# Where a phase's extremes are multiplied and reduced in a chain of selective scans

## The chip, the cores and the metric

The kernel runs on one core of a Trainium2 chip. The time is the device time of one execution in microseconds, and the median of several executions is what counts. All data are 32-bit floats.

## What is computed

The reference takes `x` (32 sequences of 750 steps with 64 channels) through three state-space layers, then an attention block and a mixture of 16 experts. Only the layers matter here. Cut down:

```python
def _ssm_layer(x, A_log, Dp, W_dbc, W_dt, b_dt):
    A = -jnp.exp(A_log)
    dbc = jnp.einsum('ble,ce->blc', x, W_dbc)
    delta, Bm, Cm = jnp.split(dbc, [DT_RANK, DT_RANK + N_STATE], axis=-1)
    delta = jax.nn.softplus(jnp.einsum('blr,er->ble', delta, W_dt) + b_dt)
    dA = jnp.exp(delta[..., None] * A)
    dBx = (delta * x)[..., None] * Bm[:, :, None, :]
    ...
    y = jnp.einsum('blen,bln->ble', hs, Cm)
    return y + Dp * x
```

`hs` is the scan `h = dA * h + dBx` along the sequence, for 64 states per channel; behind each of the first two layers pairs of neighbouring steps are averaged.

## The kernel before, in words

Two sequences at a time lie on the 128 partitions (64 channels each). A **unit** is 750 columns of such a pair (748 in layer 2). There are 28 units, grouped into 8 **phases** of four units (two in the last two phases): phases 0 to 3 are layer 0, 4 and 5 layer 1, 6 and 7 layer 2.

States whose decay is so strong that `exp` gives zero need no scan: their sum is one quadratic form of the input. For each phase the kernel finds out which states those are. It needs the smallest delta of the phase, and so the **extremes** of the first projection (row 0 of `W_dbc`): TensorE multiplies half units (375 columns) by `w0pm`, whose columns hold the projection and its negative (`extreme_rows`, matmul at L515), VectorE reduces to a maximum per partition (`extremes`, L1320), TensorE transposes that column into one row (`extremes_row`, L573), VectorE reduces it (`extremes_of_row`, L1325 and L1326), TensorE spreads it (`extremes_spread`, L577), and `lowest`, ScalarE's `bounds`, `classes` and `picks` follow. The slow states that are left, up to two, are scanned; a loop for more (`more_slots`) is skipped at run time when there are none.

The work on a unit n, by engine:

- TensorE: `mixed` (the quadratic form's product, L493 and L494 with `quad`), `summed` (a sum over channels of `PT`, L493 and L494 with `work,packed`), `weighted_b` (the mixed input B x for scan j into `pairs[1 + j]`, L493 and L494 with `big,work`), `rows` (the rows of C for unit n+1 and of delta for unit n+3 into `bank[0]`, L530 and L536), `sums` (the pooled sum of both scans, L566).
- VectorE: `load` (L1379, mixed input by `u`), `product` (L1358), `by_delta` (L1364), the scan `recur` (L1386), `output` (L1371), `read` (L1398, state by the row of C), each for 750 columns; `load`, `recur` and `read` twice a unit.
- ScalarE: softplus in parts (L965 to L979), `decay` (L990, one for each scan), `rows_out` (L1034, the rows from `bank[0]` to SBUF), `sums_out` (L1041).
- GpSimd: the rest of delta, `u`, and the pooled sums.
- SyncE: for each unit it writes the rows to DRAM (L399) and reads them back, spread over 64 partitions: `z_row` (L408) for delta, `c_rows` (L415) for C.

Each engine works its own list in the order in which `period(n)` writes it, once for n = -2 to 27; semaphores tie the lists together, and a waiting instruction holds everything behind it on its engine. PSUM is four pairs of two banks: `bank[0]` and `bank[1]` are pair 0 (`bank[0]` serves the rows and all small products of the phase chain), `pairs[1]` and `pairs[2]` hold the two scans, `pairs[3]` the quadratic form. Before, `extreme_rows` wrote into `pairs[1]`, which scan 0 of the next unit needs too.

`chain(n)` gives for a unit n the phase p that comes next and the place q of n in its own phase. With q = 0 (units 0, 4, 8, 12, 16, 20) the extremes of the next phase are made in that period; q = 1 and q = 2 carry the rest of the chain. `new` says that n is the first unit of a phase other than the first. In a new period TensorE's list opened with

```python
                if new:
                    pe.wait_ge(more_v, MV[last_of(n - 1) + 1])
                    summed(n + 1)
```

and in a period with q = 0 it went on, behind the rows, with

```python
                if q == 0:
                    pe.wait_ge(hc_v, STATIC * n + 1)
                    extreme_rows(p, pairs[1]).then_inc(dec_p, 1)
                    pe.wait_ge(rw_a, EVENT_AT[n + 1])
                ...
                if q == 0:
                    extremes_row(p)
                    weighted_b(n + 1, 0)
```

`extremes_row` waits for VectorE's reduction, so `weighted_b(n + 1, 0)`, and `mixed(n + 2)` behind it, did too.

Of the kernel before, what the change touches and what calls it, by code (L numbers as in the profile page):

```python
# [81 lines left out]
def program(nc, a, out):  # L82
    SCALE = float(D) ** 0.25
    with ExitStack() as ctx:
# [33 lines left out]
        w0pm = sb("w0pm", [128, LAYERS, 32])  # L118
# [370 lines left out]
        def _(pe):  # L489
# [19 lines left out]
            def extreme_rows(p, dst):  # L509
# [4 lines left out]
                for i in range(2 * U):  # L514
                    mm = pe.matmul(dst[32 * (i % 4):32 * (i % 4) + 32, 512 * (i // 4):512 * (i // 4) + w],  # L515
                                   w0pm[:, l, :], xcols(l, c + i * w, w), start=True, stop=True)
                return mm

            def rows(k):
# [3 lines left out]
                if c_of is not None and c_of >= Z_OF:  # L523
                    extreme_rows(NP - 1, bank[0]).then_inc(rw_p, 1)
                    return
# [6 lines left out]
                if s_of is not None:  # L532
                    _, l, w, x = unit(s_of)
                    x_ready(s_of)
                    for c in range(2):
                        mm = pe.matmul(bank[0][64 + 32 * c:96 + 32 * c, 0:w // 2], w0pm[:, l, :],  # L536
# [87 lines left out]
            def period(n):  # L624
# [7 lines left out]
                if new:  # L632
                    pe.wait_ge(more_v, MV[last_of(n - 1) + 1])
                    summed(n + 1)
# [16 lines left out]
                if nxt and not new:  # L651
                    summed(n + 1)
                if old is not None:
                    sums(old, 0)
                if q == 0:
                    pe.wait_ge(hc_v, STATIC * n + 1)
                    extreme_rows(p, pairs[1]).then_inc(dec_p, 1)
                    pe.wait_ge(rw_a, EVENT_AT[n + 1])
                elif q == 1:
# [5 lines left out]
                if s is not None:  # L665
                    pe.wait_ge(rw_a, EVENT_AT[n + 1])
                    extreme_rows(s, pairs[1]).then_inc(dec_p, 1)
# [15 lines left out]
                if nxt and q != 0:  # L683
# [11 lines left out]
                if q == 0:  # L695
                    extremes_row(p)
                    weighted_b(n + 1, 0)
# [568 lines left out]
        def _(v):  # L1266
            v.sem_inc(more_v, 1)

            def setup():
# [6 lines left out]
                for k in range(2):  # L1276
                    blk = slice(64 * k, 64 * k + 64)
                    v.tensor_copy(w0pm[blk, :, k], w0[blk, :])
                    v.tensor_scalar(w0pm[blk, :, 2 + k], w0[blk, :], -1.0, None, ALU.mult)
# [31 lines left out]
            def extremes(p):  # L1311
                l, _, U = PHASES[p]
                w = WIDTH[l] // 2
                if p == NP - 1:
                    v.wait_ge(rw_a, EVENT_AT[LAST - 1])
                    src = bank[0][:, 0:w]
                else:
                    v.wait_ge(dec_p, DP[p] + 1)
                    src = pairs[1][:, :].rearrange("p (b t) -> p b t", b=2)[:, 0:U // 2, 0:w]
                v.tensor_reduce(smx[:, :], src, AXX if p == NP - 1 else AXXY, ALU.max).then_inc(dec_v, 1)  # L1320

            def extremes_of_row(p):
                v.wait_ge(dec_p, DP[p] + 2)
                row = bank[0][0:1, 0:128].rearrange("p (g c) -> p g c", c=32)
                v.tensor_reduce(sext[:, 0:1], row[:, :, 0:2], AXXY, ALU.max, negate=True)  # L1325
                v.tensor_reduce(sext[:, 1:2], row[:, :, 2:4], AXXY, ALU.max).then_inc(dec_v, 1)  # L1326
# [105 lines left out]
            def period(n):  # L1432
# [35 lines left out]
                elif nxt:  # L1468
                    by_delta(n + 1)
                if here:  # L1470
                    recur(n, 1)
                if q == 0:
# [464 lines left out]
```

## Time and profile before

| | us |
|---|---|
| median of 3 executions | 789.09 (788.72 to 789.63) |
| the profiled execution, its own time | 790.49 |
| its span, first to last instruction | 788.7 |
| TensorE busy in the span | 713.2 (90%) |
| VectorE busy in the span | 545.3 (69%) |
| ScalarE busy in the span | 425.2 (54%) |
| GpSimd busy in the span | 439.4 (56%) |
| mean granted TensorE clock | 0.968 of full |

Busy shares are means over the whole span: the scans take the first 330 us or so, the attention and the experts the rest. Lines in the profile are lines of the kernel before. Of a 32-bit product the trace holds two passes, so a matmul of the program stands there as two (x2). Starts of instructions in the timeline overlap the ends of the ones ahead on the same engine by some tenths of a microsecond, so the distance from start to start is what a step takes.

### The profile page before, as it was taken

The page shows a single profiled execution, that of the slowest core. Times are in us where ns is not written, and L with a number is a line of the kernel's source. Part 1 is how long each engine was busy: PE and PEld are TensorE (multiplying, and loading weights), DVE is VectorE, ACT ScalarE, POOL GpSimd, SP SyncE. Part 2 cuts the span into 40 slices and gives each one's busy share as a digit, 9 for nine tenths or more (in the row PEclk, how much of TensorE's full clock was granted, in tenths as well). Part 3 has the DMA queues.
Part 4 walks back from the last instruction along what each step waited for, and adds up shares of the span by engine and source line. Part 5 has one row for each costly group of instructions (what it writes and reads, how often), then busy time and mean ns, then how long its engine had stood idle before and what let it go on. Part 6 is the DMA issues. An engine that isn't in the chain of part 4 may idle for free.

```text
span 788.7 us, 11097 instructions
## 1 busy us (share of the span) xinstructions
PE 713.2 (90%) x3474; PEld 355.5 (45%) x3474; DVE 545.3 (69%) x859; ACT 425.2 (54%) x763; POOL 439.4 (56%) x402
## 2 busy tenths in 40 slices
PE   5689998989989895848999999889999999999997
PEld 2335444544545452326777777623333333333332
DVE  3389899999999898585588888485444444454543
ACT  1678777878687874543545554443434334343332
POOL 1368777877877765735666666233444344443440
PEclk9699999999999998688999999989999999999999
DMA  4346554434545553124000000552954334443400
GB/s 130 126 122 155 152 147 124 131 83 121 129 121 123 125 134 81 39 62 86 1 2 4 3 4 4 109 107 55 209 108 99 82 83 105 106 92 79 97 1 20
DMA packets 30098, 70.20 MB, mean 89 GB/s; under 512 B 4483, under 2 KB 20175, under 8 KB 29647
## 3 DMA queue, kind: packets, MB, share of 16 engines
q1 hardware_dynamic: 29727, 68.77, 36.7%
q8 instruction: 31, 0.51, 0.3%
q10 hardware_dynamic: 304, 0.63, 0.2%
q14 instruction: 36, 0.29, 0.1%
HBM read 66.96 MB, written 2.43 MB: 88 GB/s over the span
## 4 chain that ended last, share of the span: by engine, by line
PE 46%; DVE 8%; issue 1%; ACT 1%; DVEq 0%; ACTq 0%
PE pair L834 22%; PE pair L915 11%; PE pair L775 4%; PE pair L758 3%; PE pair L811 2%; PE pair L798 1%; DVE big L1526 1%; PE pair L820 1%; PE pair L826 1%; DVE big L1530 1%; DVE big L1592 0%; DVE big L1591 0%; DVE big L1538 0%; DVE big L1531 0%; DVE big L1846 0%
## 5 line engine op out<-in xcount | busy, mean ns | idle before, releaser
L1689 DVE TENSOR_TENSOR hidden<-pair,tmp 128x502 f32<-128x502 f32 (+1 forms) x192 | 121.6, 675 | 130.1 <-PE pair L834 105.2
L1820 POOL TENSOR_TENSOR hidden<-xs,big 128x502 f32<-128x502 f32 (+1 forms) x96 | 111.8, 1166 | 166.0 <-PE pair L834 145.7
L1242 ACT ACTIVATE tmp<-pair 128x502 f32<-128x502 f32 (+1 forms) x192 | 102.4, 586 | 157.0 <-PE pair L834 157.0
L1846 POOL TENSOR_TENSOR big<-big 94x512 f32<-94x512 f32 (+3 forms) x120 | 89.2, 777 | 56.5 <-DVE big L1591 56.5
L834 PE MATMUL pair<-xs,w 64*128 64x502 f32 (+1 forms) x384 | 107.1, 634 | 0.0
L834 PE MATMUL pair<-hidden,w 64*128 64x502 f32 (+1 forms) x384 | 98.7, 590 | 4.0 <-DVE hidden L1689 3.1
L1386 DVE TENSOR_TENSOR_SCAN pair<-tmp,pair 128x750 f32<-128x750 f32 (+1 forms) x56 | 95.9, 1712 | 0.4
L1711 POOL TENSOR_TENSOR big<-big,work 128x750 f32<-128x750 f32 (+1 forms) x28 | 45.7, 1632 | 88.7 <-ACT big L973 88.7
L915 PE MATMUL pair<-hidden,w 128*64 128x502 f32 (+1 forms) x384 | 92.3, 603 | 0.0
L493 PE MATMUL pair<-big,work 128*128 128x512 f32 x112 | 61.3, 629 | 2.8 <-DVE work L1398 2.8
L834 PEld LDWEIGHTS pair<-hidden,w 64*128 64x128 f32 x384 | 36.8, 188 | 51.1 <-issue 46.5
L834 PEld LDWEIGHTS pair<-xs,w 64*128 64x128 f32 x384 | 29.2, 185 | 66.1 <-issue 36.6
L1379 DVE TENSOR_TENSOR pair<-pair,big 128x750 f32<-128x750 f32 (+1 forms) x56 | 52.1, 930 | 1.4 <-PE pair L494 0.5
L915 PEld LDWEIGHTS pair<-hidden,w 128*64 128x64 f32 x384 | 23.7, 138 | 63.3 <-DVE hidden L1689 34.6
L990 ACT ACTIVATE tmp<-big,picked 128x749 f32<-128x749 f32 (+2 forms) x56 | 49.6, 909 | 2.5 <-issue 2.4
L1714 POOL TENSOR_TENSOR work<-work 128x750 f32<-128x750 f32 (+1 forms) x28 | 46.2, 1649 | 3.0 <-ACT work L979 3.0
L1721 POOL TENSOR_TENSOR big<-big 128x750 f32<-128x750 f32 (+1 forms) x28 | 46.7, 1667 | 1.7 <-issue 0.9
L1716 POOL TENSOR_TENSOR big<-big,work 128x750 f32<-128x750 f32 (+1 forms) x28 | 46.1, 1646 | 2.2
L775 PEld LDWEIGHTS pair<-big 93*120 93x120 f32 (+1 forms) x384 | 42.2, 184 | 2.9 <-issue 1.2
L775 PE MATMUL pair<-big 93*120 93x65 f32 (+1 forms) x384 | 42.6, 268 | 0.0
L811 PE MATMUL pair<-big 120*64 120x188 f32 x384 | 34.1, 326 | 6.7 <-issue 3.8
L493 PE MATMUL pair<-big,quad 128*128 128x512 f32 x56 | 32.6, 666 | 6.4 <-DVE work L1371 5.4
(189 smaller groups left out, 1241.3 us busy)
## 6 DMA issues: line engine op xcount, KB each, us to landing
big<-dispatched SPq DMA_DIRECT2D x40, 502.0 KB, 6.6
spread<-rowsd SPq DMA_DIRECT2D x48, 375.0 KB, 5.7
spread<-rowsd SPq DMA_DIRECT2D x48, 187.5 KB, 3.4
big<-in_x SPq DMA_DIRECT2D x12, 375.0 KB, 6.3
big<-dispatched SPq DMA_DIRECT2D x8, 498.0 KB, 5.8
spread<-rowsd SPq DMA_DIRECT2D x8, 374.0 KB, 4.9
w<-in_w SPq DMA_DIRECT2D x5, 512.0 KB, 7.0
big<-in_x SPq DMA_DIRECT2D x1, 1500.0 KB, 7.2
```

Of the source, the lines that this page charges most:

```text
L493: pe.matmul(dst[:, 0:512], lhsT, rhs[:, 0:512], start=True, stop=True)
L775: mm = pe.matmul(bank[4 + n % 2][0:FT, at:at + 65], kF[r % 2][0:rows, unit, FT * f:FT * f + FT], qkv[r % 2][0:rows, unit, 143:208], start= ...
L811: mm = pe.matmul(dst[64 * b:64 * b + 64, TOK * k:TOK * k + TOK], kvm[n % 2][:, k, FTN * b + f, :], qT[n % 2][:, f, TOK * b:TOK * b + TOK], ...
L834: pe.matmul(dst[:, 0:hi - lo], weights[blk, HID * e:HID * e + HID], x[blk, :], start=True, stop=True)\
L915: mm = pe.matmul(bank[4][64 * b:64 * b + 64, 0:hi - lo], w3[:, e, :], hidT[(2 * expert + b) % 8][:, 0:hi - lo], start=(e == 0), stop=(e == ...
L990: act.activation(seqs(dA[j], l)[:, :, 1:], seqs(of(delta, n), l)[:, :, 1:], ACT.Exp, scale=picked[p % 2][:, j:j + 1]).then_inc(dk_a, 1)
L1242: act.activation(sT[i % 4][:, 0:w], bank[BANK1[i]][:, 0:w], ACT.Silu).then_inc(silu_a, 1)
L1379: v.tensor_tensor(bu, bu, of(u, n), ALU.mult).then_inc(bu_v, 1)
L1386: v.tensor_tensor_scan(h, dA[j][:, 0:w], h, 0.0, ALU.mult, ALU.add).then_inc(sc_v, 1)
L1689: v.tensor_tensor(hidT[i % 8][:, 0:hi - lo], bank[BANK2[i]][:, 0:hi - lo], sT[i % 4][:, 0:hi - lo], ALU.mult)\
L1820: pool.tensor_tensor(xw[e % 4][:, 0:hi - lo], xs[:, lo:hi], wx[:, e, 0:hi - lo], ALU.mult)\
L1846: ins = eng.tensor_tensor(dst[:, :, at:at + H * m].rearrange("p u (h d) -> p u h d", d=m), t[:, :, :, 0:m], t[:, :, :, k:D], ALU.mult)
```

## The change

The table `w0pm` grows from 32 to 34 columns a layer. The projection now stands in columns 2 and 3, its negative in 6 and 7. Read from column 2 on, a product gives rows 0, 1 (projection) and 4, 5 (negative); read from column 0 on, rows 2, 3 and 6, 7. `extreme_rows` uses that: the first four half units of a phase go to the four quarters of 32 partitions of `bank[0]` with the first form, the other four are added into the same quarters with the second. All eight half units then lie in one bank of 375 columns, eight rows a quarter, where before they lay in two banks, 750 columns, four rows a quarter. The reduction and the one behind it read accordingly.

TensorE's list: `extreme_rows` in a period with q = 0 now waits until ScalarE has copied the rows out of `bank[0]`; `weighted_b(n + 1, 0)` goes ahead of `extremes_row`; in a new period with q = 0 `rows` goes ahead of `summed(n + 1)`. VectorE's list: with q = 0 `by_delta(n + 1)` moves behind the second scan.

```diff
-        w0pm = sb("w0pm", [128, LAYERS, 32])
+
+        w0pm = sb("w0pm", [128, LAYERS, 34])
...
-            def extreme_rows(p, dst):
+            def extreme_rows(p):
+
                 l, c, U = PHASES[p]
                 w = WIDTH[l] // 2
                 for n in range(UB[p], UB[p + 1]):
                     x_ready(n)
                 for i in range(2 * U):
-                    mm = pe.matmul(dst[32 * (i % 4):32 * (i % 4) + 32, 512 * (i // 4):512 * (i // 4) + w],
-                                   w0pm[:, l, :], xcols(l, c + i * w, w), start=True, stop=True)
+                    at = 2 - 2 * (i // 4)
+                    mm = pe.matmul(bank[0][32 * (i % 4):32 * (i % 4) + 32, 0:w], w0pm[:, l, at:at + 32],
+                                   xcols(l, c + i * w, w), start=(i < 4), stop=(i >= 2 * U - 4))
                 return mm
...
                 if new:
                     pe.wait_ge(more_v, MV[last_of(n - 1) + 1])
-                    summed(n + 1)
+                    if q != 0:
+                        summed(n + 1)
...
-                if nxt and not new:
+                if nxt and (not new or q == 0):
                     summed(n + 1)
                 if old is not None:
                     sums(old, 0)
                 if q == 0:
-                    pe.wait_ge(hc_v, STATIC * n + 1)
-                    extreme_rows(p, pairs[1]).then_inc(dec_p, 1)
                     pe.wait_ge(rw_a, EVENT_AT[n + 1])
+                    extreme_rows(p).then_inc(dec_p, 1)
...
-                if nxt and q != 0:
+                if nxt:
                     weighted_b(n + 1, 0)
...
                 if q == 0:
                     extremes_row(p)
-                    weighted_b(n + 1, 0)
...
-                    v.tensor_copy(w0pm[blk, :, k], w0[blk, :])
-                    v.tensor_scalar(w0pm[blk, :, 2 + k], w0[blk, :], -1.0, None, ALU.mult)
+                    v.tensor_copy(w0pm[blk, :, 2 + k], w0[blk, :])
+                    v.tensor_scalar(w0pm[blk, :, 6 + k], w0[blk, :], -1.0, None, ALU.mult)
...
-                    src = bank[0][:, 0:w]
                 else:
                     v.wait_ge(dec_p, DP[p] + 1)
-                    src = pairs[1][:, :].rearrange("p (b t) -> p b t", b=2)[:, 0:U // 2, 0:w]
-                v.tensor_reduce(smx[:, :], src, AXX if p == NP - 1 else AXXY, ALU.max).then_inc(dec_v, 1)
+                v.tensor_reduce(smx[:, :], bank[0][:, 0:w], AXX, ALU.max).then_inc(dec_v, 1)
...
                 if k == 1:
                     classes(NP - 1)
-                elif nxt:
+                elif nxt and q != 0:
                     by_delta(n + 1)
                 if here:
                     recur(n, 1)
+                if q == 0:
+                    by_delta(n + 1)
                 if q == 0:
                     extremes(p)
```

TensorE's list at the first period of phase 1 (unit 4). `work,packed` is `summed`, `rowsel` and `w0pm ... x2` the rows, `w0pm ... x8` the extremes, `big,work` the mixed input, `packed,smx` is `extremes_row`, `big,quad` is `mixed`. Before:

```order
L493 MATMUL pair<-work,packed 128x512
L494 MATMUL pair<-work,packed 128x238
L530 MATMUL pair<-big,rowsel 32x375 x2
L536 MATMUL pair<-big,w0pm 32x375 x2
L515 MATMUL pair<-big,w0pm 32x375 x8
L573 MATMUL pair<-packed,smx 1x128
L493 MATMUL pair<-big,work 128x512
L494 MATMUL pair<-big,work 128x238
L493 MATMUL pair<-big,quad 128x512
L494 MATMUL pair<-big,quad 128x238
```

The same place now, where the lines of the kernel have moved by one to three:

```order
L533 MATMUL pair<-big,rowsel 32x375 x2
L539 MATMUL pair<-big,w0pm 32x375 x2
L494 MATMUL pair<-work,packed 128x512
L495 MATMUL pair<-work,packed 128x238
L518 MATMUL pair<-big,w0pm 32x375 x8
L494 MATMUL pair<-big,work 128x512
L495 MATMUL pair<-big,work 128x238
L576 MATMUL pair<-packed,smx 1x128
L494 MATMUL pair<-big,quad 128x512
L495 MATMUL pair<-big,quad 128x238
```

Two things moved: the rows are ahead of `summed`, and the mixed input is ahead of `extremes_row`. At unit 0 only the second did.

VectorE's list at the same period, from the first `read` (`tmp<-pair,spread`) to the output (`work<-pair,packed,big`); L1386 is the scan. Before:

```order
L1398 TENSOR_TENSOR tmp<-pair,spread 128x750
L1364 TENSOR_TENSOR pair<-pair,big 128x750
L1386 SCALAR_TENSOR_TENSOR pair<-tmp,pair 128x750
L1320 TENSOR_REDUCE smx<-pair 128x1
L1371 SCALAR_TENSOR_TENSOR work<-pair,packed,big 128x750
```

The same place now:

```order
L1398 TENSOR_TENSOR tmp<-pair,spread 128x750
L1386 SCALAR_TENSOR_TENSOR pair<-tmp,pair 128x750
L1364 TENSOR_TENSOR pair<-pair,big 128x750
L1320 TENSOR_REDUCE smx<-pair 128x1
L1371 SCALAR_TENSOR_TENSOR work<-pair,packed,big 128x750
```

`by_delta` has gone behind the scan.

## Rows read from the trace of the kernel before

**Rows 1.** The page, busy tenths of the span in 40 slices.
```profile
DVE  3389899999999898585588888485444444454543
...
PEclk9699999999999998688999999989999999999999
```

**Rows 2.** Table by stretch: length, busy us (instructions) by engine, clock, DMA.
```profile
107.00:310.00 203.00, 186.79 (x740) 95.58 (x739) 189.59 (x225) 152.00 (x243) 153.49 (x113) 1.00 0.48 120
```

**Rows 3.** Waits of VectorE by cause: us in total, times, longest us.
```profile
DVE work L1398 <- DMA spread<-rowsd: 6.9, 6, 2.0
```

**Rows 4.** The tile `smx`: durations in ns (min/median/max), and who waited for L1320.
```profile
L1320 DVE TENSOR_REDUCE smx<-pair x8: 520/911/937, 18.4 to 303.9; 128x1 f32<-128x750 f32 x6, 128x1 f32<-128x374 f32 x2
...
  PE pair L573: 11.9, 7
```

**Rows 5.** Timeline at unit 0: start us, us, engine, line [idle before, releaser].
```profile
41.86 0.93 DVE L1398 TENSOR_TENSOR tmp<-pair,spread 128x750 f32<-128x750 f32 x1
...
42.84 1.47 PE L515 MATMUL pair<-big,w0pm 128*32 128x375 f32 x16
...
43.63 0.95 DVE L1364 TENSOR_TENSOR pair<-pair,big 128x750 f32<-128x750 f32 x1 [0.84 <-POOL big L1716]
...
47.17 0.38 PE L573 MATMUL pair<-packed,smx 128*1 128x128 f32 x2 [2.86 <-DVE smx L1320]
...
49.19 1.91 PE L493 MATMUL pair<-big,quad 128*128 128x512 f32 x2
...
51.93 0.94 DVE L1358 TENSOR_TENSOR work<-pair,big 128x750 f32<-128x750 f32 x1 [1.55 <-PE pair L494]
...
55.49 0.93 DVE L1398 TENSOR_TENSOR work<-pair,spread 128x750 f32<-128x750 f32 x1
```

**Rows 6.** The tile `spread`, C rows of unit 1, then unit 5's.
```profile
L415 SPq DMA_DIRECT2D spread<-rowsd x2: 597/597/597, 45.1 to 45.7; - x2
...
DMA to landing us min/median/max: 4.8/5.3/5.8
...
DMA to landing us min/median/max: 5.3/6.2/7.2
```

**Rows 7.** Timeline at unit 4 and the start of unit 5.
```profile
85.32 1.02 PE L493 MATMUL pair<-work,packed 128*128 128x512 f32 x2
...
86.67 0.51 PE L530 MATMUL pair<-big,rowsel 128*32 128x375 f32 x2
...
86.69 0.92 ACT L990 ACTIVATE tmp<-big,picked 128x749 f32<-128x749 f32 x1 [0.70 <-issue]
...
86.78 0.95 DVE L1364 TENSOR_TENSOR pair<-pair,big 128x750 f32<-128x750 f32 x1 [0.80 <-PE pair L494]
...
87.57 0.48 ACT L1034 ACTIVATE rows<-pair 128x375 f32<-128x375 f32 x1
...
87.65 1.72 DVE L1386 TENSOR_TENSOR_SCAN pair<-tmp,pair 128x750 f32<-128x750 f32 x1
...
90.34 0.38 PE L573 MATMUL pair<-packed,smx 128*1 128x128 f32 x2 [1.57 <-DVE smx L1320]
...
92.02 1.02 PE L493 MATMUL pair<-big,quad 128*128 128x512 f32 x2
...
92.22 0.95 DVE L1379 TENSOR_TENSOR pair<-pair,big 128x750 f32<-128x750 f32 x1
...
93.47 0.94 DVE L1358 TENSOR_TENSOR work<-pair,big 128x750 f32<-128x750 f32 x1 [0.31 <-PE pair L494]
...
99.15 0.94 DVE L1398 TENSOR_TENSOR work<-pair,spread 128x750 f32<-128x750 f32 x1 [2.03 <-DMA spread<-rowsd]
```

**Rows 8.** Timeline, ScalarE's row copies at units 8 and 20.
```profile
131.41 0.48 ACT L1034 ACTIVATE rows<-pair 128x375 f32<-128x375 f32 x1 [0.18 <-PE pair L536]
...
258.96 0.48 ACT L1034 ACTIVATE rows<-pair 128x375 f32<-128x375 f32 x1 [0.20 <-PE pair L536]
```

**Rows 9.** Timeline, ScalarE before the first unit.
```profile
20.39 1.00 ACT L967 ACTIVATE work<-spread,packed,wdtc 128x750 f32<-128x750 f32 x1
```

More of the change, by code:

```diff
@@ L523, in rows @@
                 if c_of is not None and c_of >= Z_OF:
-                    extreme_rows(NP - 1, bank[0]).then_inc(rw_p, 1)
+                    extreme_rows(NP - 1).then_inc(rw_p, 1)
                     return
@@ L535, in rows @@
                     for c in range(2):
-                        mm = pe.matmul(bank[0][64 + 32 * c:96 + 32 * c, 0:w // 2], w0pm[:, l, :],
+                        mm = pe.matmul(bank[0][64 + 32 * c:96 + 32 * c, 0:w // 2], w0pm[:, l, 2:34],
                                        x[:, w // 2 * c:w // 2 * c + w // 2], start=True, stop=True)
@@ L666, in period @@
                     pe.wait_ge(rw_a, EVENT_AT[n + 1])
-                    extreme_rows(s, pairs[1]).then_inc(dec_p, 1)
+                    extreme_rows(s).then_inc(dec_p, 1)
                     extremes_row(s)
@@ L1315, in extremes @@
                     v.wait_ge(rw_a, EVENT_AT[LAST - 1])
-                    src = bank[0][:, 0:w]
                 else:
                     v.wait_ge(dec_p, DP[p] + 1)
-                    src = pairs[1][:, :].rearrange("p (b t) -> p b t", b=2)[:, 0:U // 2, 0:w]
-                v.tensor_reduce(smx[:, :], src, AXX if p == NP - 1 else AXXY, ALU.max).then_inc(dec_v, 1)
+                v.tensor_reduce(smx[:, :], bank[0][:, 0:w], AXX, ALU.max).then_inc(dec_v, 1)
             def extremes_of_row(p):
                 v.wait_ge(dec_p, DP[p] + 2)
-                row = bank[0][0:1, 0:128].rearrange("p (g c) -> p g c", c=32)
-                v.tensor_reduce(sext[:, 0:1], row[:, :, 0:2], AXXY, ALU.max, negate=True)
-                v.tensor_reduce(sext[:, 1:2], row[:, :, 2:4], AXXY, ALU.max).then_inc(dec_v, 1)
+                row, U = bank[0][0:1, 0:128].rearrange("p (g c) -> p g c", c=32), PHASES[p][2]
+                v.tensor_reduce(sext[:, 0:1], row[:, :, 0:U], AXXY, ALU.max, negate=True)
+                v.tensor_reduce(sext[:, 1:2], row[:, :, 4:4 + U], AXXY, ALU.max).then_inc(dec_v, 1)
             def lowest(p):
```

## The prediction

> **What bounds the kernel now.** The page comes first. In the 40 slices VectorE stands at 8 or 9 tenths from the third slice up to about 310 us, which is the stretch of the scans; behind that it falls to half, and nothing of the change lies there [rows 1]. The table by stretch says it with numbers: from 107 to 310 us VectorE is busy 189.59 of 203 us, TensorE 186.79, at a granted clock of 1.00 [rows 2]. So in the scans VectorE's own list of work sets the pace, and what can be won is (a) work taken off VectorE and (b) the few stretches in which it stands. Among its waits by cause stands one on the DMA that spreads the C rows, before `read`: 6.9 us in 6 times, the longest 2.0 us [rows 3]. A few large waits make up such a sum, so I looked for each of them in the timeline.
>
> The instruction that the change is about is the reduction of a phase's extremes, L1320: 8 times, 911 ns in the middle and 520 ns at its shortest; TensorE waited for it 11.9 us in 7 times [rows 4]. TensorE is not the bound, so these 11.9 us are no gain by themselves; what counts is where they make VectorE wait afterwards. The timeline answers differently for the first unit and for the five later ones.
>
> *Unit 0* [rows 5]. `read` starts at 41.86; VectorE then stands 0.84 us for GpSimd's delta, does `by_delta` (43.63), the scan, the reduction, the output. TensorE has sat 2.86 us when L573 begins at 47.17. Only then does the next unit's mixed input follow, then the quadratic product, whose first part takes 1.91 us for two passes where the same form takes 1.02 us at unit 4 [rows 7]: the granted clock has fallen to its lower level (1.2 of 2.4 GHz) behind that idle time. VectorE waits 1.55 us for it at 51.93; `read` of unit 1 follows at 55.49.
>
> *Units 4, 8, 12, 16, 20*, the first of a later phase; unit 4 stands for all [rows 7]. VectorE waits 0.80 us for `summed` (86.78), the scan starts at 87.65, and the wait before `product` is 0.31 us. Then, 5.7 us behind `product`, comes the large one: `read` of the next unit stands 2.03 us for the C rows (99.15). In the other four phases it stands 0.74, 0.98, 1.44 and 1.48 us; these five and one more small one are the 6.9 us of [rows 3].
>
> **The change part by part.**
>
> *1. Reduction over 375 columns in place of 750.* It has the size of the 374-column ones, 520 ns for 911: 0.39 us less on VectorE [rows 4], six times (before the first unit and at units 0, 4, 8, 12, 16; unit 20's phase has two units and was 374 already). The first of the six gives nothing: ScalarE's ReLU of the first softplus runs from 20.39 to 21.4 whatever the reduction does, and the bounds that use the result come behind it on ScalarE's queue [rows 9].
>
> *2. `by_delta` behind the second scan.* The scan no longer stands behind it. It still needs its decay from ScalarE.
>
> *3. The extremes' products go to the rows' bank,* so they wait until ScalarE has copied the rows out, and pair 1 stays free: the next unit's mixed input need not wait for the reduction. The same 8 matmuls, and the same 16 passes; 1.47 us at unit 0 [rows 5], taken as unchanged.
>
> *4. In a new phase the rows' matmuls go ahead of `summed`.*
>
> Sum at **unit 0**. The scan can start 0.85 us behind `read`, at 42.71, since its decay was made before 43 us. From a scan's start to the load that follows took 4.57 us (87.65 to 92.22, [rows 7]); now 0.87 us more for `by_delta` (86.78 to 87.65), 0.39 us less for the reduction, and 0.85 us to `product`: 5.90 us. `product` at 48.61 instead of 51.93: **3.3 us**. It needs the quadratic product, which goes out behind the output at about 46.5 and takes 1.4 us at full clock, so 0.6 us is spare. TensorE's idle time shrinks: rows' copy done at 41.8, extremes 42.84 to 44.3, mixed input to 45.7, L573 at 45.7. Next in line is `read` of unit 1, 3.56 us behind `product`, so 52.17; its C rows land 5.8 us behind the second issue at 45.7, at 51.5 [rows 6]. They keep 0.7 us. Were they as slow as at unit 4, 7.2 us, they would land at 52.9 and the gain would be 2.6 us. The other chains stand behind VectorE from there (ScalarE's next row copy follows `lowest`), so the shift holds to unit 4.
>
> Bounds for unit 0: nothing, if a chain that doesn't hang on VectorE holds unit 1; 3.3 us above. I take 3.3, since every issue that unit 1 needs is seen in the rows with its time.
>
> Sum at **units 4 to 20**. The 0.80 us wait goes, but the scan starts no earlier: its decay is ScalarE's L990, 86.69 to 87.61 [rows 7]. In the scan's place VectorE now waits for ScalarE, and `by_delta` comes behind, uncovered. `product` comes 5.90 us behind 87.65, at 93.55, against 93.47: 0.1 us late, and the 2.03 us wait on the C rows covers it. So everything here hangs on those rows. Their copy to SBUF, L1034, stands behind the same decay: it began at 87.57, without a wait. Sending TensorE's rows 1.35 us earlier (86.67 would become 85.32) brings nothing at unit 4. At unit 8 ScalarE waited 0.18 us for them, at unit 20 0.20 us [rows 8], at unit 16 about 0.1 us, at unit 12 nothing. These fractions are all that can come through: with the overlap of two rows, about 0.2 us in three phases, **0.6 us**. Bounds: nothing, or 1.35 us a phase if the decay moved too, capped by each wait (1.35, 0.74, 0.98, 1.35, 1.35: 5.8 us).
>
> The extremes now end later. `summed` ends at 87.6, the copy at 88.05, the products at 89.5; the reduction's turn is at 90.15. 0.6 us to spare; so that new wait costs nothing.
>
> **Sum**: 3.3 + 0.6 = 3.9 us, rounded to 4.0. The profiled execution took 790.49 us with a span of 788.7, 1.4 us above the median of 789.09 (788.72 to 789.63). Its own time would become 786.5, the median **785.1 us**.
>
> A word on the clock. At unit 0 the lower level came behind 2.86 us without a matmul [rows 5]; at unit 4 TensorE sat 1.57 us before L573 [rows 7], and in the later phases, which have the same order of work, the clock stayed at 1.00 [rows 2]. In the new order the wait before L573 shrinks and one of 0.5 us comes in between `summed` and the extremes. The Trainium skill (TensorE: Matmul & The Clock Gate, section "What's actually happening") calls the lower level the default and says that activity lifts it. By that rule alone a phase whose matmuls are spread thinner could fall to it, which is rival C and would make about 791.8 of the sum's 785.1; unit 0 agrees with the rule, units 4 to 20 with their 1.57 us show no fall.
>
> **The rivals.**
>
> *A. Unit 0 gives less.* Either the clock falls there again, and the quadratic product takes 2.7 us as in [rows 5] (46.6 to 49.3, `product` 0.7 us later than the sum), or the C rows land late. Both give 2.6 us: 2.6 to 3.2 with the rest, about 786.2. For: both costs are in rows. Against: the idle time is gone.
>
> *B. The rows do get out early in new phases.* 3.3 + 5.8 = 9.1 us: 780.0. For: the wait is the DMA's, and TensorE's part moves by 1.35 us. Against: ScalarE's order is unchanged and it is busy until 87.57.
>
> *C. Slower.* The clock falls in each of the five phases. Then the mixed input and the quadratic product, one behind the other, take 2.7 us each for 1.4; less the spare 0.6 us, 2.0 us a phase. Of these 10 us up to 6.7 (five waits) can be hidden, if the row chain isn't held up. Net of 3.9: from 0.6 faster to 6 slower, middle 791.8. It becomes slower than before at 0.8 us exposed a phase. Against: TensorE idled 1.57 us at unit 4 before [rows 7], and from 107 us on, four phases of the same order, the clock was 1.00 [rows 2].
>
> *D. No change.* The shift of unit 0 is lost before unit 4, because the DMA of rows or x holds a chain of its own; the waits on C rows grow by it. 788.5. Against: from unit 1 to 4 VectorE never waits for a DMA.
>
> **How the numbers follow.** Under 0.2% (1.6 us) a measurement of this kernel can't tell from no change. Forecast 0.60, A 0.19, B 0.06, C 0.06, D 0.09. Faster: forecast, A and B, 0.85. Same: D, 0.09. Slower: C, 0.06. The forecast's own spread is about 1 us either way (three runs spread by 0.9 us). The range takes in the forecast and A with that spread, 783.6 to 787.4, and leaves out B, C and D.
>
> **What would show it.** In the profile after: the reduction at about 0.52 us in all eight; at unit 0 no wait of VectorE between the first `read` and the next unit's, no lower clock near 49 us, `read` of unit 1 near 52.2; at units 4 to 20 a wait of 0.8 to 1.7 us before the second scan with ScalarE as its cause, and still a wait on the C rows of 0.6 to 1.9 us. It is wrong if the C row waits are gone (B), if the granted clock falls in a new phase (C), or if unit 4 starts as late as before (D).

## The result and the profile after

The change makes the kernel faster: a median of 783.87 us (781.48 to 785.51, 6 executions) beside 788.99 us (787.61 to 790.23, 6 executions) on the same chip, a ratio of 0.9928 with a 95% interval of 0.9913 to 0.9944. Of 789.09 us that is 783.4 us. The forecast was 785.1 us with a range from 783.6 to 787.4. The direction was right, the gain was under-sized: 5.7 us where 4.0 stood, just outside the range.

| us | before | after |
|---|---|---|
| the profiled execution, its own time | 790.49 | 784.34 |
| its span | 788.7 | 782.5 |
| TensorE busy | 713.2 | 712.7 |
| VectorE busy | 545.3 | 542.2 |
| mean granted TensorE clock | 0.968 | 0.972 |

The page of the kernel after, VectorE and the granted clock in 40 slices; it answers to [rows 1]:

```profile
DVE  3399899999999997585588888494544445454543
...
PEclk9699999999999997788999999999999999999999
```

The slices of the scans look as before; the gain isn't to be seen at this grain. It shows in four views. First the tile `smx` of the kernel after, durations in ns (min/median/max), beside [rows 4]:

```profile
L1320 DVE TENSOR_REDUCE smx<-pair x8: 520/537/548, 18.4 to 299.6; 128x1 f32<-128x375 f32 x6, 128x1 f32<-128x374 f32 x2
...
  PEld pair L576: 4.7, 8
  PE pair L576: 1.3, 3
```

The same view of the kernel before has, beside the 11.9 us of its matmuls, a row for the weight loads:

```profile
  PEld pair L573: 2.5, 2
```

All eight reductions are short, and TensorE waits 6.0 us for them (weight loads 4.7, matmuls 1.3) where it waited 14.4 (2.5 and 11.9). Then VectorE's waits by cause (us in total, times, longest), beside [rows 3]:

```profile
DVE work L1398 <- DMA spread<-rowsd: 7.4, 7, 2.0
DVE pair L1386 <- ACT tmp L992: 5.7, 5, 1.7
```

The waits on the C rows are all still there, and a new row has come: five times the second scan waits for ScalarE's decay. Unit 0 in the timeline of the kernel after (start us, us, engine, line [idle before, releaser]), beside [rows 5]:

```profile
41.74 0.93 DVE L1398 TENSOR_TENSOR tmp<-pair,spread 128x750 f32<-128x750 f32 x1
...
42.53 1.47 PE L518 MATMUL pair<-big,w0pm 128*32 128x375 f32 x16
...
42.59 1.71 DVE L1386 TENSOR_TENSOR_SCAN pair<-tmp,pair 128x750 f32<-128x750 f32 x1
...
45.04 0.54 DVE L1320 TENSOR_REDUCE smx<-pair 128x1 f32<-128x375 f32 x1
...
45.63 0.38 PE L576 MATMUL pair<-packed,smx 128*1 128x128 f32 x2 [0.17 <-DVE smx L1320]
...
46.63 1.10 PE L494 MATMUL pair<-big,quad 128*128 128x512 f32 x2 [0.62 <-DVE work L1371]
...
48.26 0.92 DVE L1358 TENSOR_TENSOR work<-pair,big 128x750 f32<-128x750 f32 x1
...
52.47 0.94 DVE L1398 TENSOR_TENSOR work<-pair,spread 128x750 f32<-128x750 f32 x1 [0.56 <-DMA spread<-rowsd]
```

From the first `read` to `product` are 6.52 us now (41.74 to 48.26); they were 10.07 (41.86 to 51.93). The quadratic product takes 1.10 us: the clock has not fallen. `read` of unit 1 then stands 0.56 us for its C rows. And unit 4, beside [rows 7]:

```profile
82.23 0.51 PE L533 MATMUL pair<-big,rowsel 128*32 128x375 f32 x2
...
82.86 0.94 DVE L1398 TENSOR_TENSOR tmp<-pair,spread 128x750 f32<-128x750 f32 x1 [0.90 <-DMA spread<-rowsd]
83.00 1.12 PE L494 MATMUL pair<-work,packed 128*128 128x512 f32 x2
83.52 0.92 ACT L992 ACTIVATE tmp<-big,picked 128x749 f32<-128x749 f32 x1 [0.69 <-issue]
84.34 0.46 ACT L1036 ACTIVATE rows<-pair 128x375 f32<-128x375 f32 x1
84.47 1.72 DVE L1386 TENSOR_TENSOR_SCAN pair<-tmp,pair 128x750 f32<-128x750 f32 x1 [0.67 <-ACT tmp L992]
84.86 1.47 PE L518 MATMUL pair<-big,w0pm 128*32 128x375 f32 x16 [0.33 <-ACT rows L1036]
...
86.26 1.13 PE L494 MATMUL pair<-big,work 128*128 128x512 f32 x2
86.93 0.54 DVE L1320 TENSOR_REDUCE smx<-pair 128x1 f32<-128x375 f32 x1
...
90.15 0.92 DVE L1358 TENSOR_TENSOR work<-pair,big 128x750 f32<-128x750 f32 x1
...
95.72 0.94 DVE L1398 TENSOR_TENSOR work<-pair,spread 128x750 f32<-128x750 f32 x1 [1.95 <-DMA spread<-rowsd]
```

The rows are ready early and lie there: they end at about 83.1, and ScalarE copies them at 84.34, behind its decay. The wait for the C rows is 1.95 us, as large as the 2.03 before.

### The profile page after: what moved, and what is told of

Same layout as the page of the kernel before. It is cut to its first block, busy times and chain, and to the rows that moved or that the text cites. A ratio compares the mean times of both kernels' runs of the same rounds, so it can differ in the third digit from the quotient of the medians.

```text
span 782.5 us, 11086 instructions
## 1 busy us (share of the span) xinstructions
PE 712.7 (91%) x3474; PEld 353.6 (45%) x3474; DVE 542.2 (69%) x859; ACT 424.6 (54%) x763; POOL 439.5 (56%) x402
## 4 chain that ended last, share of the span: by engine, by line
PE 46%; DVE 8%; issue 1%; ACT 1%; DVEq 0%; ACTq 0%
PE pair L836 22%; PE pair L917 11%; PE pair L777 5%; PE pair L760 3%; PE pair L813 2%; PE pair L800 1%; PE pair L822 1%; PE pair L828 1%; DVE big L1528 1%; DVE big L1532 1%; DVE big L1594 0%; DVE big L1593 0%; DVE big L1540 0%; DVE big L1533 0%; DVE big L1848 0%
## 5 line engine op out<-in xcount | busy, mean ns | idle before, releaser
L1386 DVE TENSOR_TENSOR_SCAN pair<-tmp,pair 128x750 f32<-128x750 f32 (+1 forms) x56 | 95.8, 1712 | 6.0 <-ACT tmp L992 5.7
L1713 POOL TENSOR_TENSOR big<-big,work 128x750 f32<-128x750 f32 (+1 forms) x28 | 45.7, 1631 | 84.4 <-ACT big L975 84.4
L813 PE MATMUL pair<-big 120*64 120x188 f32 x384 | 36.0, 338 | 5.5 <-issue 3.8
```

The source lines that it names most:

```text
L813: mm = pe.matmul(dst[64 * b:64 * b + 64, TOK * k:TOK * k + TOK], kvm[n % 2][:, k, FTN * b + f, :], qT[n % 2][:, f, TOK * b:TOK * b + TOK], ...
L1386: v.tensor_tensor_scan(h, dA[j][:, 0:w], h, 0.0, ALU.mult, ALU.add).then_inc(sc_v, 1)
```

## The experiments

The theory at the start: unit 0 gives 3.3 us by its order, the new phases only the fractions that ScalarE stood for the rows. Two measures per profile tell rivals apart, and both are read from starts in the timeline: the time from the output of unit 0 to that of unit 4 (**unit 0's stretch**), and in each new phase the time from a unit's output to ScalarE's row copy (**the copy's distance**), 8.62 us in all five phases of the kernel before.

**1. The bank alone.** The changed kernel with the three moves undone; what is left is the reduction over 375 columns.

```diff
-                    if q != 0:
-                        summed(n + 1)
+                    summed(n + 1)
...
-                if nxt:
+                if nxt and q != 0:
                     weighted_b(n + 1, 0)
...
                     extremes_row(p)
+                    weighted_b(n + 1, 0)
...
-                elif nxt and q != 0:
+                elif nxt:
                     by_delta(n + 1)
```

> The changed kernel with all three moves undone: only the extremes in the rows' bank and the reduction over 375 columns stay; the mixed input again behind extremes_row, by_delta ahead of the scan, summed ahead of the rows. Theory (the gain is the mixed input freed at unit 0): unit 0 gives the 0.4 us of the shorter reduction, the five new phases nothing, since the extremes now wait for the row copy; about 788.6, the scans 0.4 to 0.8 us shorter than before. Rival (the bank and the shorter reduction are what counts): more than half of the 5 us is here, under 786.5.

Measured: 788.36 us (12 executions) beside 790.28, a ratio of 0.9978 (0.9962 to 0.9994), so 1.7 us. The clock fell at 47.2 us in its profile, unit 0's stretch is 42.62 us, and the copy's distance stayed at 8.62. The shorter reduction by itself gives little, as expected; the moves carry the rest.

**2. `summed` first again in new phases.**

```diff
-                    if q != 0:
-                        summed(n + 1)
+                    summed(n + 1)
...
-                if nxt and (not new or q == 0):
+                if nxt and not new:
                     summed(n + 1)
```

> The changed kernel with summed ahead of the rows again in new phases. Theory (ScalarE's decay holds the row copy, so TensorE's rows going first brings at most the 0.1 to 0.2 us that ScalarE waited): 0.3 to 0.7 us slower than the changed kernel over the scans, C row waits as in it. Rival (rows first is what won the extra microsecond over the prediction): the scans 1 us or more longer than in the changed kernel.

Measured: 784.87 us beside 790.28, 0.9940 (0.9920 to 0.9961). The copy's distance is 8.62 in all five phases again, where the changed kernel has 8.56, 8.34, 8.61, 8.39 and 8.33. Putting the rows ahead therefore brings 0.06 + 0.28 + 0.01 + 0.23 + 0.29 = 0.87 us in all. The times of the two kernels don't separate; the distances do, since they repeat to 0.01 us. (One thing more differs in this profile, far behind the scans; it is taken up with the table by stretch below.) Unit 4 in the timeline of this experiment shows why it is so little:

```profile
83.13 0.92 ACT L991 ACTIVATE tmp<-big,picked 128x749 f32<-128x749 f32 x1 [0.70 <-issue]
...
84.01 0.48 ACT L1035 ACTIVATE rows<-pair 128x375 f32<-128x375 f32 x1
```

The copy stands behind the decay here as it does in the changed kernel, with no wait of its own.

**3. `by_delta` ahead of the second scan again.**

```diff
-                elif nxt and q != 0:
+                elif nxt:
                     by_delta(n + 1)
...
-                if q == 0:
-                    by_delta(n + 1)
```

> The changed kernel with by_delta ahead of the second scan again. Theory: unit 0 gets the wait for GpSimd's delta back and loses 0.9 us of its 3.2; the new phases neither gain nor lose, what VectorE does is hidden by the wait on the C rows; scans about 0.9 us longer than in the changed kernel. Rival (by_delta behind the scan costs in new phases what it wins at unit 0): no difference or faster.

Measured: 784.87 us (12 executions) beside 790.28, 0.9940 (0.9920 to 0.9960): not to be told from the changed kernel. At unit 4 of its profile VectorE waits 1.63 us for `summed`, the scan starts 9.64 us behind the unit's output (8.69 in the changed kernel), and yet `product` comes nearly as early: 14.46 us behind the output (76.20 to 90.66), against 14.37 (75.78 to 90.15) in the changed kernel and 14.52 before. From the first `read` the distances are 8.24 and 7.29 us, but that is because in the changed kernel this `read` itself stood 0.90 us for its C rows. In all five phases the move is worth 0.05 to 0.33 us at `product`, 1.05 us in sum, and the wait on the C rows takes that back. The prediction had the move neutral for this reason, no gain at `product`, and it holds to a third of a microsecond. At unit 0 `product` comes 7.24 us behind the first `read` where the changed kernel has 6.52, but `read` of unit 1 comes 10.78 us behind it against 10.73: the wait on the C rows covers the move there too. So the expectation (0.9 us lost at unit 0) missed, and its rival, no difference, held.

**4. ScalarE copies the rows ahead of the decay in new phases.** This is rival B forced: if ScalarE's order holds the rows, they get out now.

```diff
+                first = q == 0 and n > 0
+                if first:
+                    for e in range(EVENT_AT[n], EVENT_AT[n + 1]):
+                        rows_out(e)
...
-                for e in range(EVENT_AT[n], EVENT_AT[n + 1]):
-                    rows_out(e)
+                if not first:
+                    for e in range(EVENT_AT[n], EVENT_AT[n + 1]):
+                        rows_out(e)
```

> The changed kernel, and in new phases ScalarE copies the rows out before the decay of the second scan. Theory (the row copy behind the decay is what holds the C rows): the copy comes 0.9 us earlier in each of the five phases, the wait on the C rows shrinks by that and by the 0.5 us that the scan starts later; 0.9 us each at units 4, 12, 20, little at 8 and 16, together 2.8 us: about 781. Rival (the C rows are held by the DMA or by TensorE): no gain, and 0.5 us a phase lost to the later decay where the wait is short, about 785.

Measured: 780.67 us (6 executions) beside 790.28, 0.9883 (0.9863 to 0.9902): 9.2 us faster than before and about 3.4 us faster than the changed kernel (0.9883 beside 0.9928 and 0.9931; from unit 4's output to unit 24's its profile takes 209.8 us, where six profiles of the changed kernel take 213.2 on the mean). The copy's distance is 7.67, 7.43, 7.71, 7.40 and 7.42. Unit 4 in its timeline:

```profile
83.88 0.48 ACT L1036 ACTIVATE rows<-pair 128x375 f32<-128x375 f32 x1 [0.62 <-PE pair L539]
84.26 0.91 ACT L992 ACTIVATE tmp<-big,picked 128x749 f32<-128x749 f32 x1
...
85.20 1.73 DVE L1391 TENSOR_TENSOR_SCAN pair<-tmp,pair 128x750 f32<-128x750 f32 x1 [1.76 <-ACT tmp L992]
...
95.06 0.94 DVE L1403 TENSOR_TENSOR work<-pair,spread 128x750 f32<-128x750 f32 x1 [0.56 <-DMA spread<-rowsd]
```

The second scan now waits 1.76 us for its decay, and the wait for the C rows falls from 1.95 to 0.56 (to nothing in three of the five phases, to 0.26 in one). That the row chain through ScalarE holds the new phases is thereby shown.

**5. The new order at unit 0 alone**, with the bank and the short reduction everywhere. `summed` stands first in every new phase as in experiment 2, and:

```diff
-                if nxt:
+                if nxt and (q != 0 or n == 0):
                     weighted_b(n + 1, 0)
...
                     extremes_row(p)
+                    if n > 0:
+                        weighted_b(n + 1, 0)
...
-                elif nxt and q != 0:
+                elif nxt and n != 0:
                     by_delta(n + 1)
...
-                if q == 0:
+                if n == 0:
                     by_delta(n + 1)
```

> The changed kernel with all moves undone in the new phases (4, 8, 12, 16, 20): the mixed input ahead of extremes_row and by_delta behind the scan at unit 0 alone; the rows' bank and the short reduction stay everywhere. Theory (unit 0 is the change): scans 3 to 4 us shorter than before, within 0.8 us of the changed kernel. Rival (the new phases' new order carries a share of its own): less than 3 us.

Measured: 785.99 us (12 executions) beside 790.11, 0.9942 (0.9913 to 0.9970), 4.6 us (2.4 to 6.9). By the median most of the gain comes with unit 0; the interval leaves open how much of it. But its profile surprised me. At unit 0:

```profile
46.13 0.38 PE L576 MATMUL pair<-packed,smx 128*1 128x128 f32 x2 [1.11 <-DVE smx L1321]
...
47.13 1.79 PE L494 MATMUL pair<-big,quad 128*128 128x512 f32 x2 [0.62 <-DVE work L1372]
...
49.75 0.94 DVE L1359 TENSOR_TENSOR work<-pair,big 128x750 f32<-128x750 f32 x1 [0.93 <-PE pair L495]
```

The same order as in the changed kernel, and the clock fell at 47.4 all the same. The idle time before L576 is 1.11 us here because VectorE's first `read` stood 0.84 us for its C rows, so that the reduction came later. Experiment 2 has 1.07 us at this place, from a first `read` 0.80 us late, and no fall. Unit 0's stretch is 41.49 us, between the two kernels. From unit 0's output to unit 24's the scans take 256.8 us in this profile, 1.5 less than on the mean before and 4.3 more than in the changed kernel, so the 3 to 4 us expected are not in it. So the clock at this place is not settled by the order alone, and one profile isn't enough to say what it costs.

**6. The order before, with TensorE's idle time filled** by two products of 512 columns that nobody reads.

```diff
+                if n == 0:
+                    for _ in range(2):
+                        pe.matmul(bank[1][:, 0:512], blocks, unit(0)[3][:, 0:512], start=True, stop=True)
```

> The kernel before, with two products of 512 columns added to TensorE's list at unit 0 ahead of extremes_row (their result in bank 1 is overwritten unused), in the idle time of 2.9 us. Theory (part of unit 0's loss is the lower clock behind that idle time, 1.3 us where only the quadratic product meets it and up to 2.5 us where the mixed input does too): the clock doesn't fall near 46 to 49 us, the time from unit 0's output to unit 4's is 40.9 to 41.2 us in place of 42.4 to 44.2. Rival (the loss is the order alone, the clock costs VectorE nothing): 42.4 us or more.

Measured: 788.06 us (12 executions) beside 789.69, 0.9978 (0.9958 to 0.9999), so 1.7 us (0.1 to 3.3) from work that does nothing. Unit 0 in its timeline:

```profile
45.33 1.98 PE L697 MATMUL pair<-big,packed 128*128 128x512 f32 x4
...
47.92 0.38 PE L573 MATMUL pair<-packed,smx 128*1 128x128 f32 x2 [0.60 <-DVE smx L1323]
...
49.59 1.02 PE L493 MATMUL pair<-big,quad 128*128 128x512 f32 x2
...
51.05 0.94 DVE L1361 TENSOR_TENSOR work<-pair,big 128x750 f32<-128x750 f32 x1 [0.31 <-PE pair L494]
```

The idle time is 0.60 us where it was 2.86 [rows 5], the clock doesn't fall, and the wait at `product` is 0.31 where it was 1.55. The Trainium skill (TensorE: Matmul & The Clock Gate, section "What's actually happening") says that activity releases the throttle, and the filler agrees. Unit 0's stretch is 41.37 us, so the rival (42.4 or more, the clock costs VectorE nothing) fell.

**7. Both kernels again and again**, to see how unit 0's stretch spreads. Six more profiles of the kernel before and five of the changed one, unedited, on four chips. The changed kernel was also timed once more.

> The changed kernel once more, nothing edited. Theory (the change is worth about 4.2 us in the scans, and 1.5 us more of the first result came from where TensorE's clock happened to be at its lower level behind the scans): a ratio near 0.9945 (784.7 at 789.1), the profile's scans 4.0 to 4.6 us shorter than before, and the stretch behind them another length than in the first profile of it. Rival (the 1.5 us belong to the change): again 0.993 or lower, and the stretch from 507 to 568 us shorter by 2.4 us in this profile too.

> The kernel before once more, for a second profile of it. Theory: the scans as long as in the first within 0.5 us, the stretch between the ninth and the tenth write of the residual (506.77 to 567.95 in the first profile, 61.2 us) anything from 58.5 to 61.2 us, by whether the clock falls in it. Rival: 61.2 us again.

> The kernel before, a third profile. From unit 0's output to unit 4's took 42.4 and 44.2 us in the first two. Theory (that difference is how early the clock falls): 42 to 44.5 us, with the low clock beginning between 45 and 49 us. Rival (the second profile was a stray): 42.4 us.

> The changed kernel, a third profile. Theory: 39.3 to 39.5 us from unit 0's output to unit 4's as in both so far, the row copies of the new phases 8.56, 8.34, 8.61, 8.39 and 8.33 us behind the output to the hundredth, the C rows 9.9 to 11.5 us behind those copies. Rival: other copy times, so that they hang on something that varies.

> The kernel before, a fourth profile, for the same question as the third: 42 to 44.5 us from unit 0's output to unit 4's by the theory, 42.4 by the rival; and in the experts 61.2 us between the ninth and tenth write of the residual where the clock falls there, 58.7 where not.

> The kernel before, fifth profile. If the 1.9 us between the ninth and the tenth write of the residual (59.9 to 61.2 us in four profiles of before, 58.8 in three of the changed kernel) are luck of the clock, about one profile in two of before shows 58.8; if they belong to the change, none does. Unit 0 to unit 4: 42.4 to 44.3 us.

> The changed kernel, fourth profile. Luck: sometimes 59.5 to 61 us in that stretch. The change's own: 58.8 again. Unit 0 to unit 4: 39.3 to 39.5 us.

The pairs that followed (15 to 18) repeated the last two. Measured: 784.06 us (10 executions) beside 790.11 for the changed kernel, 0.9931 (0.9901 to 0.9960), and by stretch in the 7 and 6 profiles:

| us, mean (lowest to highest) | before, 7 | after, 6 | difference |
|---|---|---|---|
| output of unit 0 to that of unit 4 | 42.94 (40.98 to 44.25) | 39.28 (38.81 to 39.80) | 3.7 |
| output of unit 4 to that of unit 24 | 215.3 (213.8 to 217.2) | 213.2 (212.2 to 214.2) | 2.1 |
| unit 24 to the ninth write of `resid` | 212.8 | 212.6 | 0.3 |
| ninth to tenth write of `resid`, the experts' start | 60.5 (59.5 to 61.4) | 58.8 (58.7 to 58.8) | 1.7 |
| tenth to last write of `resid` | 216.0 | 216.0 | 0.0 |

Unit 0's stretch doesn't overlap between the kernels, and it spreads by 3.3 us before and by 1.0 after. Of what was expected, the copy's distances came back to the hundredth, and the experts' start took 58.8 us in each profile of the changed kernel, so the rival of the first of these expectations held; two ranges were too narrow, 42.4 to 44.3 us (the fifth profile has 40.98) and, where the clock doesn't fall in the experts, 58.7 (the fourth has 59.8). The extremes of the kernel before show what spreads. The third of its profiles:

```profile
47.20 0.58 PE L573 MATMUL pair<-packed,smx 128*1 128x128 f32 x2 [2.77 <-DVE smx L1320]
47.72 2.08 PE L493 MATMUL pair<-big,work 128*128 128x512 f32 x2
...
50.38 1.91 PE L493 MATMUL pair<-big,quad 128*128 128x512 f32 x2
50.62 0.95 DVE L1379 TENSOR_TENSOR pair<-pair,big 128x750 f32<-128x750 f32 x1 [1.68 <-PE pair L494]
```

The low level began at 46.5 us and held through both products, so that the mixed input was slow too, 2.08 us for the 1.13 of [rows 5]. And the fifth profile of the same kernel:

```profile
46.97 0.38 PE L573 MATMUL pair<-packed,smx 128*1 128x128 f32 x2 [2.68 <-DVE smx L1320]
47.28 1.12 PE L493 MATMUL pair<-big,work 128*128 128x512 f32 x2
...
48.64 1.02 PE L493 MATMUL pair<-big,quad 128*128 128x512 f32 x2
48.84 0.95 DVE L1379 TENSOR_TENSOR pair<-pair,big 128x750 f32<-128x750 f32 x1
50.10 0.94 DVE L1358 TENSOR_TENSOR work<-pair,big 128x750 f32<-128x750 f32 x1 [0.31 <-PE pair L494]
```

The same code, 2.68 us idle, and no fall at all; the stretch is 40.98 us, the shortest of the seven. So the stretch divides into an order's part and a clock's part. Order: 40.98 (no fall) or 41.37 (filled), less 39.28, is 1.7 to 2.1 us. Clock: the mean of 42.94, less 40.98 or 41.37, is 1.6 to 2.0 us. These stretches also hold waits of the first `read` for its C rows (0.90 us in the filled one, 0 in the fifth profile). The distance from the first `read` to `product` holds none, and it says much the same: 6.51 or 6.52 us in all six profiles of the changed kernel, 8.12 filled, 8.27 without a fall, and 9.69 to 11.15 in the six with one. That is 1.6 to 1.8 us for the order and, in the same code, nothing or 1.4 to 2.9 us for the clock. In six of the seven profiles of the kernel before the low level came between 45.7 and 48.5 us; in none of the six of the changed kernel did it come between 36 and 300 us.

**8. Experiment 4 with `by_delta` ahead of the scan again in the new phases**, so that VectorE has something to do while it waits for the decay.

```diff
-                elif nxt and q != 0:
+                elif nxt and n != 0:
                     by_delta(n + 1)
...
-                if q == 0:
+                if n == 0:
                     by_delta(n + 1)
```

> ScalarE's row copy ahead of the decay in new phases, as in the run before this that did so, and by_delta ahead of the second scan again at units 4 to 20, where the decay is late now. Theory: VectorE does by_delta while it waits for the decay; 0.5 us each where the wait on the C rows no longer covers it (units 8 to 20), so 1 to 1.5 us less than that run in the scans, about 779.5. Rival (summed ends too late for it): no difference.

Measured: 781.14 us (6 executions) beside 790.11, 0.9885 (0.9841 to 0.9930): not to be told from experiment 4. The 1 to 1.5 us expected are not there. In its profile the `read` behind unit 4's `product` stands 2.33 us for C rows; it comes 12.75 us behind their copy. The other four phases take between 0.70 us less and 0.04 us more than in experiment 4. Experiment 4 and this one are the fastest kernels of the study.

## Why the prediction was right or wrong

**The direction and the first place: right.** Unit 0 is the largest single term, 3.7 us on the mean, and each step there came as said: the scan at 42.59 (42.71 forecast), no wait from the first `read` to `product`, `product` at 48.26 (48.61), the reduction at 0.54 us. `read` of unit 1 came at 52.47, for the 52.17 of the text, because the C rows were the last to come after all; the 0.7 us that they were to keep was gone, as the text feared.

**The new phases: the mechanism was right, the term was short.** The scans wait for ScalarE's decay 0.67, 0.38, 1.71, 1.50 and 1.43 us (0.8 to 1.7 forecast, so two are shorter), the C row waits stay at 0.54 to 1.95, and the rows' earlier place brings 0.87 us where 0.6 stood. Experiment 4 shows that the reason given, the copy behind the decay, is right. But over the profiles the stretch of these phases is 2.1 us shorter on the mean, against the 0.6 of the sum. What lies beyond the 0.87 is not settled: from row copy to `read` the chain of DMAs takes from 9.9 to 12.1 us in both kernels alike, its five means add up to 54.4 us before and 53.4 after, and phase by phase they differ in both directions.

**The step that failed is the term that the sum put at nothing: "behind that it falls to half, and nothing of the change lies there".** No instruction of the change lies behind the scans; but the experts' start takes 59.5 to 61.4 us before and 58.7 to 58.8 after, 1.7 us less on the mean. That is as much as the 5.7 us measured exceed the 4.0 forecast, though the profiles' terms don't add up well enough to call it the whole miss. The table by stretch (length, busy us (instructions) of TensorE, weight load, VectorE, ScalarE, GpSimd, then clock, DMA), before and then after:

```profile
506.80:567.90 61.10, 56.15 (x237) 18.90 (x236) 35.72 (x72) 26.35 (x47) 25.57 (x22) 0.94 0.63 126
```

```profile
503.20:562.00 58.80, 53.50 (x239) 18.51 (x237) 36.12 (x72) 26.35 (x47) 25.57 (x22) 1.00 0.67 133
```

The same work with the clock at 0.94 and at 1.00. In four of the seven profiles of the kernel before the clock fell between 510.7 and 521.5 us (61.1 us on the mean), in none of the six after. Where it didn't fall the kernel before still took 59.7 us, 0.9 more. There GpSimd starts its first product of the experts later; the fifth profile of the kernel before, then the first of the changed kernel:

```profile
510.00 4.52 POOL L1820 TENSOR_TENSOR hidden<-xs,big 128x502 f32<-128x502 f32 x4 [16.71 <-DMA big<-dispatched]
```

```profile
505.48 4.53 POOL L1822 TENSOR_TENSOR hidden<-xs,big 128x502 f32<-128x502 f32 x4 [15.77 <-DMA big<-dispatched]
```

That is 3.17 and 2.24 us behind the ninth write of `resid` (506.83 and 503.24). GpSimd waits for the second of eight loads `big<-dispatched`, which land one behind the other, mostly 2.4 to 2.5 us apart. One of the first seven lands 3.3 to 3.7 us behind the one ahead of it, and which one goes with a DMA packet that isn't data. It stands in the view of DMA queues, here from 504.5 to 506 us in the same profile of the kernel before and from 514 to 515.5 us in that of the changed kernel (packets, MB, share):

```profile
q8 instruction: 1, 0.02, 5.4%
```

```profile
q8 instruction: 1, 0.02, 5.3%
```

The packet has 16 KB. In all twenty profiles, with its start and the stretch in us:

| start of the packet behind the ninth write | late load | clock | experts' start | profiles |
|---|---|---|---|---|
| 11.0 to 11.1 | seventh | no fall | 58.5 to 58.8 | the changed kernel, 6; experiments 3, 4, 8 |
| 0.3 to 0.8 | third | falls | 61.1 to 61.4 | the kernel before, 3; experiment 1 |
| 0.7 | second | falls | 60.5 | experiment 2 |
| -1.7 | second | falls | 60.5 | the kernel before, 1 |
| -1.8 to -1.7 | second | no fall | 59.5 to 59.8 | the kernel before, 3; experiment 5 |
| -1.7 | second | short fall | 58.3 | experiment 6 |

What the nine profiles of the first row share and the other eleven lack is one of the three moves, the rows ahead of `summed` in new phases. Experiment 2 undoes that one alone, in TensorE's list, and has the packet at 0.7 us, a fall and 60.5 us; the edits of experiments 3, 4 and 8 to VectorE's and ScalarE's lists leave the packet at 11.1. So this term belongs to the change and is not luck. The chain from packet to late load to clock is read from twenty profiles that agree; no run moved the packet by itself, and why the clock falls behind an early packet in some executions and not in others stays open.

**The 3.3 us of unit 0 were near the mark, but were read off one profile.** The waits in them are real, yet part of them is what the clock cost in that one execution. Over seven profiles the stretch costs 42.94 us and not the 42.36 of the profile that I had, and what the change wins on the mean is 3.7 us. The text took the 1.55 us wait and the 1.91 us product of [rows 5] as the cost of the low clock; the runs show this cost from nothing to about 3 us in the same code. That 3.3 came so close is luck in part.

**The range was too narrow.** Three executions within 0.9 us were taken as the spread of the whole. Single executions of the kernel before went from 785.35 to 797.26 us, and the terms above spread by 3.3, 3.4 and 1.8 us. The terms of the table add up to 7.8 us, much like the difference of the profiled executions (790.4 and 782.8 us on the mean); the timed comparisons give 5.7 and 5.5 us. Seven and six profiles, from several chips, don't bear a sum to better than a microsecond or two, so the terms of the table are good for their order and not for their last digit.

**The rivals.** A (unit 0 gives less) fell, 3.7 us on the mean; its mechanism, the clock falling there again, was seen once, in experiment 5. B fell for the changed kernel, and experiment 4 made it true: 780.67 us for the 780.0 that it gave, with 5.5 us in the new phases (215.3 on the mean before, 209.8) for its 5.8. C fell: no low level in a new phase of the changed kernel. Two were seen in profiles of the kernel before, at 91.9 and at 263.0 us, so the danger was real, in the other kernel. There `product` came 1.9 and 1.7 us late (16.44 us behind the unit's output for 14.52, 15.79 for 14.10), and the `read` behind it no longer waited for its C rows: most of the cost was hidden, as C had reckoned for such a case. D fell: the shift of the outputs was 3.17 us at unit 4 and 4.25 at unit 24.

## What to carry to other kernels

When a wait is the price of a fallen TensorE clock, profile the same kernel several times before you cost it: the order's part repeats to some hundredths of a microsecond, the clock's part may be zero in one execution and 3 us in the next. Don't put a stretch at nothing because no line of it was edited: compare it in several profiles, its DMA queues of kind "instruction" too. Where a transfer is the last to come, follow its chain back through every engine's queue and move the step that stands first in line; here TensorE's rows went ahead of `summed` for 0.87 us in five phases, and moving ScalarE's copy ahead of one decay gave about 3.4 us. An instruction that fills an idle TensorE can pay although nobody reads it.

## What the hardware showed that I had not expected

- The low clock level behind the same idle time begins anywhere from 45.7 to 48.5 us, holds through one product or both, or doesn't come (2.68 us idle in the fifth profile, 2.86 in the first). The Trainium skill (the same page and section) says, of the change to the full clock, that its point depends on where the first matmul falls in a rhythm of the hardware that doesn't start with the kernel. No run here tests that for the fall; its spread of 2.8 us between executions of one kernel would fit.
- A transfer of instructions goes with late data: a packet of 16 KB on queue q8 goes with a load that lands 3.3 to 3.7 us behind the one ahead of it instead of about 2.45, in all twenty profiles, and an edit of the scans, more than 200 us earlier, moved it by 10 to 13 us against the experts' work.
- Two useless products of 512 columns made the kernel faster by 1.7 us (interval 0.1 to 3.3). Its one profile also has a shorter experts' start (58.3 us for 60.5 on the mean before), so not all of it need come from unit 0.
- Eight products of 375 columns took 1.47 us in the trace whether they went to two banks in pair 1 or were added into the quarters of one bank [rows 5].
- The same transfers of the C rows took from 9.9 to 12.1 us from the row copy to `read` within one kernel, more than anything the change does in a new phase.
